# Sparse experts ordered ahead of five last dense blocks, and a last stage in eight sections

## The reference

```python
x = layernorm(x + attention(x))            # 16 heads of 8, latent keys and values
S = sigmoid(x @ Wg).T                      # 8 experts x 4096 tokens
G, I = top_k(S, 1024)                      # each expert takes its 1024 best tokens
ex = x[I]                                  # gathered rows
hid = gelu(einsum('ekh,ehf->ekf', ex, W1) + b1)     # 128 -> 512
out = (einsum('ekf,efh->ekh', hid, W2) + b2) * G    # 512 -> 128
y = zeros.at[I].add(out)                   # scattered back
x = layernorm(x + y)
```

## Time and profile before

| what | value |
|---|---|
| median of 3 runs | 536.09 us (535.33 to 537.52) |
| the profiled execution | 533.78 us, its span 532.2 us |
| PE busy | 469.9 us (88% of the span) |
| POOL busy | 266.3 us (50%) |
| chain that ended last, by engine | PE 75%, DVE 11%, DMA 5%, ACT 3% |

### The profile page before, as it was taken

One profiled execution on the slowest core, in us unless ns is written; L12 is line 12 of the kernel. 1 busy time (PEld: TensorE's weight loads), 2 busy tenths in 40 slices (PEclk: granted clock), 3 DMA queues, 4 the chain that ended last, 5 costly groups with the idle time before them and its releaser, 6 DMA issues.

```text
span 532.2 us, 10902 instructions
## 1 busy us (share of the span) xinstructions
PE 469.9 (88%) x3910; PEld 384.9 (72%) x3911; DVE 330.3 (62%) x874; ACT 295.3 (55%) x587; POOL 266.3 (50%) x360
## 2 busy tenths in 40 slices
PE   5999999989999999999985788899999979999900
PEld 4777777767777777777763577789999969999900
DVE  5577776766767667677775797873223533444284
ACT  3277777757777677766763352354554433444325
POOL 9460534326333353531236400684787878786461
PEclk9999999999999999999999699899999988999965
DMA  3422233474433333233021100012333324232445
GB/s 90 79 67 55 52 76 87 112 167 71 92 87 70 73 73 77 58 82 83 23 61 43 40 16 7 24 47 56 86 57 64 43 47 62 48 35 26 85 101 156
DMA packets 47709, 35.65 MB, mean 67 GB/s; under 512 B 5704, under 2 KB 42600, under 8 KB 47656
## 3 DMA queue, kind: packets, MB, share of 16 engines
q1 hardware_dynamic: 39656, 28.18, 22.4%
q0 software_dynamic: 7552, 6.49, 8.2%
q10 hardware_dynamic: 448, 0.28, 0.3%
HBM read 12.46 MB, written 9.57 MB: 41 GB/s over the span
## 4 chain that ended last, share of the span: by engine, by line
PE 75%; DVE 11%; DMA 5%; ACT 3%; issue 2%; POOL 2%; SPq 1%; ACTq 0%; POOLq 0%; DVEq 0%
PE banks L1200 16%; PE banks L1137 12%; PE banks L1120 11%; PE banks L1100 10%; PE banks L1187 4%; PE banks L1189 4%; PE banks L1188 4%; PE banks L1051 3%; PE banks L1029 2%; DVE v_stage L1500 2%; PE banks L1075 1%; PE banks L1061 1%; PE banks L1067 1%; DVE probs L1563 1%; PE banks L1163 1%
## 5 line engine op out<-in xcount | busy, mean ns | idle before, releaser
L1347 DVE TENSOR_REDUCE row_max<-banks 128x2 f32<-128x512 f32 x256 | 166.2, 680 | 54.5 <-PE banks L1100 53.7
L891 ACT ACTIVATE probs<-banks 128x512 f32<-128x512 f32 x256 | 140.8, 595 | 28.6 <-PE banks L1120 26.9
L943 ACT ACTIVATE hT_flat<-banks,b_cols 128x512 f32<-128x512 f32 x112 | 76.7, 688 | 102.6 <-PE banks L1189 101.4
L1100 PE MATMUL banks<-k_pad,q_stack 96*128 96x256 f32 x512 | 118.3, 315 | 1.2 <-DMA k_pad<-k_lo 1.2
L1120 PE MATMUL banks<-q_stack,k_pad 100*128 100x256 f32 (+3 forms) x512 | 106.4, 289 | 5.3 <-ACT probs L891 2.1
L1200 PE MATMUL banks<-w_buf,hT_flat 128*128 128x128 f32 x896 | 108.5, 280 | 0.0
L1200 PEld LDWEIGHTS banks<-w_buf,hT_flat 128*128 128x128 f32 x896 | 106.7, 196 | 1.4
L1100 PEld LDWEIGHTS banks<-k_pad,q_stack 96*128 96x128 f32 x512 | 82.2, 197 | 9.0 <-issue 6.5
L1120 PEld LDWEIGHTS banks<-q_stack,k_pad 100*128 100x128 f32 (+3 forms) x512 | 78.8, 190 | 11.3 <-issue 7.9
L788 POOL DMA_INDIRECT summed<-v_flat,index x40 | 65.4, 1635 | 15.2 <-issue 11.3
L1137 PE MATMUL banks<-probs,v_flat 128*32 128x256 f32 x1024 | 68.5, 385 | 0.7 <-ACT probs L891 0.7
(11 more groups left out here) (230 smaller groups left out, 656.8 us busy)
## 6 DMA issues: line engine op xcount, KB each, us to landing
q_stack<-q_hi SPq DMA_DIRECT2D x32, 128.0 KB, 3.3
w_buf<-in_L_ffn_W SPq DMA_DIRECT2D x16, 256.0 KB, 3.0
k_pad<-k_hi SPq DMA_DIRECT2D x60, 64.0 KB
x_table<-rows SPq DMA_DIRECT2D x16, 136.0 KB, 2.4
rows<-in_L_attn_x SPq DMA_DIRECT2D x8, 256.0 KB, 3.1
q_stack<-q_lo SPq DMA_DIRECT2D x16, 128.0 KB, 3.4
summed<-rows SPq DMA_DIRECT2D x16, 128.0 KB, 2.8
probs<-summed SPq DMA_DIRECT2D x4, 512.0 KB, 6.0
```

The source lines that it names most:

```text
L891: s.activation(probs[:, h % 8], ps_second[:, h % 2], ACT.Exp, scale=SCALE).then_inc(exp_done, 1)
L943: s.activation(hT[:, i % 2, f], banks[:, up_bank(i, f)], ACT.Gelu, bias=b1_cols[:, FBLK * e + f:FBLK * e + f + 1]).then_inc(gelu_done, 1)
L1100: mm = t_.matmul(ps_first[:, h % 3, i * SEQ:(i + 1) * SEQ], q_stack[0:ROWS_1, n % 2, side, t, i * P:(i + 1) * P], k_pad[0:ROWS_1, n % 2, c ...
L1347: v.tensor_reduce(row_max[:, c, 2 * t:2 * t + 2], ps_first[:, h % 3].rearrange("p (i j) -> p i j", i=2), AX, ALU.max).then_inc(first_free, 1)
```

## The change

- `ORDER`: one dense block, not two, stands between sparse experts 2, 3, 4 and 5, so that five dense blocks, (d, 7, 3) to (d, 7, 7), are the last.
- `pieces_of`: in the block behind (s, e, 1) the downs of (s, e, 1) come first, and then the ups of the dense block with the turn for the next expert. In block 7, the ups come in two halves around the downs of block 6; the first half stands before `numbers_of(2)`.
- Both DRAM tables are numbered by partition: tile t, partition p is row 32 p + t. Stores and loads then move longer pieces (two tiles of a partition at a time when storing, four when loading). The token numbers of the lists are made to fit (`iota`).
- The last stage goes by eight sections of four tiles. POOL adds section q (256 KB) as soon as it is loaded and dense block (d, 7, q) is done, and it also makes the roots: one addition and one power of -0.5 for the four tiles. ACT's square root and DVE's reciprocal go. `BY_DVE` is (4, 2, 1, 1, 1, 1, 1, 2).
- On DVE: the dense results of (d, 7, 5), statistics 0 and 1, scales 0, those of (d, 7, 6), statistics 2 to 4 each with the scales before it, those of (d, 7, 7), and the rest likewise.
- Some semaphores of the start are merged, to make room for four more; the waits ask for the same events.

The diff, cut to its core:

```diff
+ORDER = ([("d", 6, c) for c in range(6)] + [("s", 0, 0), ("s", 0, 1), ("d", 6, 6), ("s", 1, 0), ("s", 1, 1), ("d", 6, 7),
+         ("s", 2, 0), ("s", 2, 1), ("d", 7, 0), ("s", 3, 0), ("s", 3, 1), ("d", 7, 1), ("s", 4, 0), ("s", 4, 1),
+         ("d", 7, 2), ("s", 5, 0), ("s", 5, 1)] + [("d", 7, c) for c in range(3, QUADS)])
+FIRST_SPARSE = AT[("s", 0, 0)]
+PAIRED = FIRST_SPARSE + 2
...
+def down_first(i):
+    return i > 0 and ORDER[i - 1][0] == "s" and ORDER[i - 1][2] == 1
...
         elif i < PAIRED:
-            parts = [part for at in (0, 2) for part in (((at, at + 1), ()), ((), (at, at + 1)))]
+            parts = [ups(i, (0, 1)), downs(i, range(4)), ups(i, (2, 3))]
+        elif down_first(i):
+            parts = [downs(i, range(4)), ups(i, range(4))]
         else:
-            parts = [(range(4), ()), ((), range(4))]
+            parts = [ups(i, range(4)), downs(i, range(4))]
...
-        summed_rows = summed.rearrange("(t p) d -> p t d", p=P)
+        summed_rows = summed.rearrange("(p t) d -> p t d", p=P)
+        x1_rows = x1_table.rearrange("(p t) g -> p t g", p=P)
...
-            g.iota(token_i[:], pattern=[[P, TILES]], base=-ID_BASE, channel_multiplier=1).then_inc(indices_set, 1)
+            g.iota(token_i[:], pattern=[[1, TILES]], base=-ID_BASE, channel_multiplier=TILES).then_inc(indices_set, 1)
...
+            def add_section(q):
                 pool.wait_ge(f_in[q], 16)
-                pool.wait_ge(dense_done, 2 * q + 2)
+                pool.wait_ge(dense_done, q + 1)
                 passed(pool, pool_waits)
+                at = slice(QT * q, QT * (q + 1))
+                g.tensor_tensor(xc_all[:, at], xc_all[:, at], rows[:, at, 0:D], ALU.add).then_inc(f_added, 1)
+            def root_section(q):
+                at = slice(QT * q, QT * (q + 1))
+                pool.wait_ge(f_averaged, QT * (q + 1))
+                g.tensor_tensor(f_sd[:, at], f_mv[:, at, 1], eps_pair[:, 0:QT], ALU.add).then_inc(f_rooted, 1)
+                pool.wait_ge(f_rooted, 2 * q + 1)
+                g.tensor_tensor(f_rstd[:, at], f_sd[:, at], minus_half[:, 0:QT], ALU.pow).then_inc(f_rooted, 1)
+            for q in range(SECTIONS):
+                add_section(q)
+                if q:
+                    root_section(q - 1)
+            root_section(SECTIONS - 1)
...
-                if part < HOT_PARTS[2] - 1:
-                    pieces(2)
+                pieces(2 if part < HOT_PARTS[2] - 1 else 1)
...
-                    if (i, 3) in TURNS_AT:
+                    if (i, 3) in TURNS_AT and not down_first(i):
                         copy_taken(TURNS_AT[(i, 3)])
                     kind, e, c = ORDER[i - 1]
                     if kind == "s":
                         give_sparse(i - 1)
                     elif e == DENSE[1]:
                         give_dense(i - 1)
+                    if (i, 3) in TURNS_AT and down_first(i):
+                        copy_taken(TURNS_AT[(i, 3)])
...
-            blocks(PAIRED, end - 2)
+            blocks(FIRST_SPARSE + 1, end - 2)
             statistics(0)
-            blocks(end - 2, end - 1)
             statistics(1)
             scales(0)
+            blocks(end - 2, end - 1)
+            for q in range(2, 5):
+                statistics(q)
+                scales(q - 1)
             blocks(end - 1, end)
-            statistics(2)
-            scales(1)
-            statistics(3)
-            scales(2)
-            scales(3)
+            for q in range(5, SECTIONS):
+                statistics(q)
+                scales(q - 1)
+            scales(SECTIONS - 1)
```

More of the change, by code:

```diff
@@ L65, with ups, downs @@
 TURN_NUMBER = {block: i for i, block in enumerate([("d", 6, c) for c in range(QUADS)] + SPARSE_BLOCKS)}
+def down_first(i):
+    return i > 0 and ORDER[i - 1][0] == "s" and ORDER[i - 1][2] == 1
 def pieces_of(n):
[L71 to L77, removed]
+    def ups(i, fs):
+        for f in fs if i < n else ():
+            yield "up", (i, f)
+            if (i, f) in TURNS_AT:
+                yield "turn", TURNS_AT[(i, f)]
+    def downs(i, cs):
         for c in cs if i else ():
@@ L82, in pieces_of @@
     for i in range(n + 1):
-        if i < FINE:
-            parts = [((f,), (f,)) for f in range(4)]
+        if i <= FIRST_SPARSE:
+            parts = [ups(i, (0, 1)), downs(i, (0, 1)), ups(i, (2, 3)), downs(i, (2, 3))]
         elif i < PAIRED:
-            parts = [part for at in (0, 2) for part in (((at, at + 1), ()), ((), (at, at + 1)))]
-        else:
-            parts = [(range(4), ()), ((), range(4))]
-        pieces += [list(items(i, fs, cs)) for fs, cs in parts]
+            parts = [ups(i, (0, 1)), downs(i, range(4)), ups(i, (2, 3))]
+        elif down_first(i):
+            parts = [downs(i, range(4)), ups(i, range(4))]
+        else:
+            parts = [ups(i, range(4)), downs(i, range(4))]
+        pieces += [list(part) for part in parts]
     return pieces
@@ L379, in post_ln_layer @@
         f_added = sem("f_added")
[L380 removed]
+        f_in = [sem(f"f_in{i}") for i in range(SECTIONS)]
         f_statted, f_averaged, f_rooted = sem("f_statted"), sem("f_averaged"), sem("f_rooted")
@@ L415, in free_down, with by_dve, tiles_by, load_section @@
                 engine.wait_ge(dense_read, c + 1)
-        BY_DVE = 2
-        QT = TILES // 4
+        BY_DVE = (4, 2, 1, 1, 1, 1, 1, 2)
+        def by_dve(section):
+            return BY_DVE[section]
+        def tiles_by(engine_is_dve, section):
+            return sum(by_dve(i) if engine_is_dve else QT - by_dve(i) for i in range(section + 1))
+        def load_section(queue, q):
+            queue.dma_start(xc_all[:, q * QT:(q + 1) * QT], summed_rows[:, q * QT:(q + 1) * QT]).then_inc(f_in[q], 16)
         def q_rows(term):
@@ L971, in normalise @@
                 act.wait_ge(f_biased, q + 1)
-                for t in range(QT * q, QT * (q + 1) - BY_DVE):
+                for t in range(QT * q, QT * (q + 1) - by_dve(q)):
                     s.activation(xc_all[:, t], xc_all[:, t], ACT.Identity, scale=f_rstd[:, t:t + 1],
                                  bias=f_bias[:, t:t + 1]).then_inc(f_done, 1)
[L976 to L982, removed]
+            for q in range(SECTIONS):
+                normalise(q)
         @block.tensor
@@ L1702, in scales @@
                 part = slice(QT * q, QT * (q + 1))
-                dve.wait_ge(f_rooted, q + 1)
-                v.reciprocal(f_rstd[:, part], f_sd[:, part]).then_inc(linked_step, 1)
-                dve.wait_ge(linked_step, linked.next())
+                dve.wait_ge(f_rooted, 2 * q + 2)
                 v.scalar_tensor_tensor(out=f_bias[:, part].unsqueeze(2), in0=f_mv[:, part, 0:1], scalar=-1.0,
                                        in1=f_rstd[:, part].unsqueeze(2), op0=ALU.mult, op1=ALU.mult).then_inc(f_biased, 1)
-                for t in range(QT * (q + 1) - BY_DVE, QT * (q + 1)):
+                for t in range(QT * (q + 1) - by_dve(q), QT * (q + 1)):
                     v.tensor_scalar(xc_all[:, t], xc_all[:, t], f_mv[:, t, 0:1], f_rstd[:, t:t + 1], ALU.subtract,
```

95 lines of the change are left out of this document (45 added, 50 removed), and 3 rows, old and new, of the table ORDER.

## The result

The changed kernel takes **540.44 us** (median of 20 runs, 537.93 to 543.87) against 536.15 us for the kernel before beside it (20 runs). The ratio is 1.0096, 95% interval 1.0072 to 1.0119: about 1% slower, where 0.2% slower was forecast. The time lies in the forecast's range and beside rival C's 541.2 us.

What follows compares the result with a forecast made beforehand. POOL was taken as full from 388 to 500 us. Last bias at 528.6 + 0.1 + 0.8 + 3.8 made a span of 533.3, 1.1 above before; added to the median 536.09, 537.2 us, range 531 to 543.

Steps and rivals of the forecast that it cites:

- rival C: Last stage: POOL and DVE obstruct each other, two dense results 1 us longer, additions 2 more in all; 541.2 us, chance 0.15.
- Part 1, the order on PE: PE's block order: last downs end at 514.8 us instead of 505.3; scatter 1 starts at 388.1 instead of 388.60.
- Five gaps, a wait and half a clock behind it: On PE: 1.9 us idle at experts 1 to 5, 3.6 us wait for expert 5's gather, then 2.9 us for half clock.
- Rival B: On PE: five 1.9 us gaps each followed by 2.9 us of half speed; PE ends at 522.8, 545.2 us, chance 0.13.
- Part 2, scatters and loads: POOL's scatters and first load: last landing 1.1 us sooner, at 500.3; data 2.1 us sooner, at 503.4; renumbered tables cost nothing.
- Part 3, the last stage: Final additions and normalisation: POOL's work 21.4 us, DVE's 20.5 us, last bias ready at 528.6, span 533.3.
- DVE waits for about 2.8 us more: Last stage: beyond its own work ending at 525.8, DVE waits 2.8 us on POOL, mostly before the last sections.
- some 0.15: Last stage on DVE: price in us of each of eight bias operations, from 0.20 holding one and a reciprocal.
- the quiet row: Dense result on DVE priced at 0.69 us, as when POOL paused, not 1.63 as during POOL's additions; sum 533.3.
- the price set aside: Contention charge not taken: results of (d, 7, 6) and (d, 7, 7) about 1 us more each, sum 535.3.
- POOL's powers are long and touch few numbers: Last stage: the reason given for pricing dense results at 0.69 us although they now meet a busy POOL.
- theory F: From the experiments: POOL's addition holds DVE instructions only with two SBUF inputs, or one input and the output in SBUF.

Runs made afterwards that it cites:

- the last version: Changed kernel with the old order and pieces, POOL only adding, roots on ACT, DVE reordered, last two dense results and negated means in PSUM: 531.19 us, ratio 0.9956.

## Why the prediction was right or wrong

- **Part 1, the order on PE: right.** Five gaps, a wait and half a clock behind it, each within 0.7 us; PE's end within 0.2. Rival B (the clock falls in every bare turn) is out: 1.00 over four of the five. The order by itself costs nothing (ratio 1.0014): with it alone PE ends 8.1 us later than before (513.43 against 505.32), and the time is the same, since POOL's scatters come sooner and the last stage gives that back.
- **Part 2, scatters and loads: right**, on the cautious side by 1.2 to 1.3 us; scatter 5 waited for scatter 4's landing, as said. Tables: nothing, measured.
- **Part 3, the last stage: the term that failed.** Its own work was priced well: POOL's string by its rows, DVE's 20.5 us, with 0.6 for two tiles behind the last product, against 26.4 - 5.7 - 1.5 = 19.2 measured (from 507.22 to that product's end at 533.64, less held time and DVE's two waits). What failed is the step "DVE waits for about 2.8 us more": it was 1.5 us of waits and 5.7 of held instructions, 7.2 in all. A second, smaller miss of 0.9 us lies between the last product and the end (5.6 us, forecast 4.7); ACT's two tiles took the 0.9 forecast, the DMA engines move nothing behind 537, and what fills the rest stays open. The misses add up: 4.4 us more of waits and holds, 1.3 less work, a start 0.5 sooner and 0.9 at the end make 3.5, and 539.2 - 2.4 - 533.3 is 3.5.
- **The step "some 0.15" for a bias product** came from a row at a moment when POOL was quiet; the product at 520.33 in the same trace, beside an addition, took twice as long. The same page of rows had the warning, 1.63 against 0.69 for a dense result, and I weighed it for the dense results only, and took the quiet row there too; the price set aside, about 1 us for each of two, was right (0.68 and 0.94). "POOL's powers are long and touch few numbers" was true: at 524.28 a dense result of two SBUF inputs takes 0.69 beside the power at 523.61. But it is the additions between the powers that hold, and the order puts one behind each root.
- **Rival C had the outcome** (0.15, 541.2 us), and its point of decision was met: the last two dense results took 2.8 us (514.18 to 516.99) and 3.1 (523.57 to 526.64), both over 2.6. Its price was in another place: additions were not 0.25 us longer than 1.38 (1.26, one of 1.49), and of 5.7 us held, 4.1 are bias products, which it did not have. That the time lies in the range is luck in part: the range's high end came from rivals B and C, and neither's sum is what happened.
- **The chance**: within 0.5% had 0.44. Slower by over 0.5% had 0.28 and is what happened; held products in the sum of part 3 would have moved the likeliest case there.

## What to carry to other kernels

When small steps move to GpSimd between long additions, write the two engines' orders side by side and ask what VectorE starts at the moment at which each addition starts; price that instruction at the addition's length if it is a product, a sum or a scaling with all operands in SBUF, however short it is alone. Put long GpSimd additions in one row and give VectorE statistics, or work with an operand in PSUM, to do beside them. When one held instruction is freed, look at the next one, which takes over the hold.

## What the hardware showed that was not expected

- The hold doesn't depend on size: 4 numbers a partition waited 1.2 us for the end of a 1.26 us addition of 512, and single-input instructions were held like those with two. The Trainium skill, GPSIMD Engine Reference, Specifications, names two cases: VectorE instructions with two SBUF inputs and those in a 2-port performance mode. I had used only the first; the one-input rows (1.20 against 0.14 us) would fit the second, which no run here shows by itself.
- Not held beside additions: operations with an operand in PSUM (0.69 at 503.21 above; 0.16 for the products; 0.70 for a dense result), statistics (0.86 for four, as when POOL is idle) and, in the last version, reciprocals (0.17 at 515.62, inside additions from 507.73 to 517.53). So "one input and the output in SBUF", the second condition of theory F, isn't the whole condition either: statistics and reciprocals have both there. Beside GpSimd's powers, two products of 512 numbers from two SBUF inputs took their usual 0.69 us (at 524.28 above, and at 521.72 with additions first, where a power runs from 521.05 to 522.07).
